# Moving two projections, their statistics and their norms by a quarter of an attention group in a four-layer kernel

## What is computed

```python
q = _split_heads(x @ Wq.T + bq)
k = _split_heads(x @ Wk.T + bk)
v = _split_heads(x @ Wv.T + bv)
scores = jnp.einsum('hbnd,hbmd->hbnm', k, q) * SCALE
attn = jax.nn.softmax(scores, axis=-1)
out = jnp.einsum('hbnm,hbmd->hbnd', attn, v)
```

## Time and profile before

| | us |
|---|---|
| median of 3 runs | 871.92 |
| lowest and highest run | 866.49, 875.07 |
| profiled execution | 876.69 |
| its span | 874.9 |

### The profile page before, as it was taken

How to read it: one execution, slowest core, us unless ns; L and a number is a source line. 1 busy time by engine, 2 the same in 40 slices (tenths; PEclk the granted TensorE clock), 3 DMA queues, 4 the chain that set the end, 5 groups by cost and what they waited for, 6 DMA issues and landing times.

```text
span 874.9 us, 13107 instructions
## 1 busy us (share of the span) xinstructions
PE 618.2 (71%) x3680; PEld 385.2 (44%) x3713; DVE 483.3 (55%) x1238; ACT 400.1 (46%) x900; POOL 365.7 (42%) x401
## 2 busy tenths in 40 slices
PE   4872109600179999930978977877978999998995
PEld 2451006300158999920968863222222233343443
DVE  4870015300036655600645677686866887867986
ACT  4420103200024666600534648555756777787651
POOL 4157750677720000075032433787477070013552
PEclk9876558855579999965879997898989999999999
DMA  8999410211102666631545645242241131000001
GB/s 270 373 247 344 169 42 1 87 54 51 48 1 72 178 172 171 180 88 42 159 119 145 166 126 150 62 138 56 52 127 54 29 104 56 1 2 0 2 12 37
DMA packets 99628, 91.52 MB, mean 105 GB/s; under 512 B 10784, under 2 KB 84608, under 8 KB 98688
## 3 DMA queue, kind: packets, MB, share of 16 engines
q1 hardware_dynamic: 90704, 75.01, 28.6%
q0 software_dynamic: 7680, 15.74, 6.2%
q10 hardware_dynamic: 1200, 0.23, 0.1%
HBM read 45.14 MB, written 45.61 MB: 104 GB/s over the span
## 4 chain that ended last, share of the span: by engine, by line
PE 46%; another core or an unknown queue 18%; DVE 14%; issue 12%; ACT 6%; DMA 2%; POOL 1%; ACTq 1%; SPq 0%; POOLq 0%; DVEq 0%
PE ps L1621 7%; PE ps L1608 6%; PE ps L1726 5%; PE ps L1736 5%; PE ps L1716 4%; DVE mx L1230 4%; PE ps L1631 3%; PE ps L1616 3%; PE ps L1530 2%; PE ps L1535 2%; ACT big L807 2%; DVE arena L1348 1%; ACT arena L773 1%; DMA dmat_s<-dmat 1%
## 5 line engine op out<-in xcount | busy, mean ns | idle before, releaser
L1230 DVE TENSOR_REDUCE mx<-ps 128x2 f32<-128x1024 f32 x128 | 151.0, 1217 | 49.5 <-PE ps L1716 37.9
L807 ACT ACTIVATE big<-ps 128x512 f32<-128x512 f32 x256 | 141.4, 598 | 67.2 <-PE ps L1726 32.7
L558 POOL DMA_INDIRECT big<-od,idx x72 | 69.0, 958 | 187.2 <-DMA od<-big 123.6
L542 POOL DMA_INDIRECT xd<-xt,idx x120 | 116.2, 968 | 69.7 <-issue 35.7
L1535 PE MATMUL ps<-arena,hmT 96*128 96x128 f32 x128 | 26.9, 343 | 125.8 <-issue 102.1
L1152 DVE TENSOR_TENSOR hm<-sg,ps 128x176 f32<-128x176 f32 x124 | 41.7, 336 | 118.1 <-ACT sg L745 74.1
L1621 PE MATMUL ps<-arena,xbT 128*128 x496 | 99.8, 325 | 4.7 <-DVE xbT L1156 2.7
L1726 PE MATMUL ps<-arena 128*128 128x512 bf16 (+1 forms) x234 | 82.6, 395 | 24.4 <-ACT big L807 11.6
L1608 PE MATMUL ps<-arena,hmT 96*128 x496 | 80.4, 286 | 26.4 <-issue 22.4
L1535 PEld LDWEIGHTS ps<-arena,hmT 96*128 96x128 f32 x128 | 21.0, 229 | 142.2 <-issue 108.0
L735 ACT ACTIVATE big<-ps 128x256 f32<-128x256 f32 x124 | 47.7, 384 | 76.2 <-PE ps L1608 47.0
(11 more groups left out here) (221 smaller groups left out, 1088.7 us busy)
## 6 DMA issues: line engine op xcount, KB each, us to landing
big<-xd SPq DMA_DIRECT2D x62, 256.0 KB
od<-big SPq DMA_DIRECT2D x62, 256.0 KB
arena<-scr SPq DMA_DIRECT2D x96, 96.0 KB
xd<-zeros SPq DMA_DIRECT2D x1, 8192.0 KB
xd<-zeros SPq DMA_DIRECT2D x1, 7680.0 KB, 30.9
arena<-w_gu SPq DMA_DIRECT2D x4, 1408.0 KB, 21.3
arena<-w_d SPq DMA_DIRECT2D x4, 768.0 KB, 17.7
scr<-places SPq DMA_DIRECT2D x8, 384.0 KB
```

Source lines behind the costliest of these rows:

```text
L542: pool.indirect_dma_start(out=xd[f], out_offset=bass.IndirectOffsetOnAxis(ap=idx[:, t, k:k + 1], axis=0), in_=xt[:, t], in_offset=None).th ...
L558: pool.indirect_dma_start(out=slot[:, k], out_offset=None, in_=od[f], in_offset=bass.IndirectOffsetOnAxis(ap=idx[:, t, k:k + 1], axis=0)). ...
L807: act.activation(ering[:, HG * (mt % 2) + h], ps[:, 4 + h % 2, :], ACT.Exp, scale=SCALE).then_inc(exp_ready, 1)
L1230: v.tensor_reduce(mx[:, k, TB * h + 2 * a:TB * h + 2 * a + 2], ps[:, 2 * a:2 * a + 2, :], AX_X, ALU.max).then_inc(s1_free, 1)
```

## The change

It moves work of sequences 2 and 3, and of those alone. Sequence 2 is projected in groups 4 and 5, sequence 3 in groups 8 and 9. "x", q, k and v each go one slot later: before (i,0) (i,1) (i,2) (i+1,0), after (i,1) (i,2) (i+1,0) (i+1,1). The statistics go from the end of the group before to behind the second row maximum of groups 4 and 8, and the norms from behind the second row maximum to behind the fifth (group 4) and the fourth (group 8). The three steps of q and of k of sequence 2 on DVE go later accordingly, and so does the DVE's copy of v. SP writes the key parts of these two sequences behind the maxima of groups 6 and 10 and no longer ahead of them. The last edit keeps PE's wait for the copied maxima in front of the first slot that is used.

```diff
--- before.py
+++ after.py
@@ -75,12 +75,15 @@
 
 
     LATER = {(0, 0): ("x", 1), (0, 1): ("q", 1), (0, 2): ("k", 1), (1, 0): ("v", 1),
-             (4, 0): ("x", 2), (4, 1): ("q", 2), (4, 2): ("k", 2), (5, 0): ("v", 2),
-             (8, 0): ("x", 3), (8, 1): ("q", 3), (8, 2): ("k", 3), (9, 0): ("v", 3)}
+             (4, 1): ("x", 2), (4, 2): ("q", 2), (5, 0): ("k", 2), (5, 1): ("v", 2),
+             (8, 1): ("x", 3), (8, 2): ("q", 3), (9, 0): ("k", 3), (9, 1): ("v", 3)}
     SLOTS = ((1, 2), (2, 2), (3, 0))
-    STATS_IN = {4: 2, 8: 3}
-    TURN_IN = {i: b for (i, _), (what, b) in LATER.items() if what == "x"}
-    PARTS_AT = ((0, 2, 1), (0, 3, 0), (0, 3, 1), (0, 3, 1), (1, 0, 0), (1, 0, 1))
+    STATS_AT = {(4, 0, 1): 2, (8, 0, 1): 3}
+    NORM_AT = {(4, 2, 0): 2, (8, 1, 1): 3}
+    V_AT = {(1, 2, 0): 1, (5, 3, 0): 2, (9, 3, 0): 3}
+    PARTS_AT = {1: ((0, 2, 1), (0, 3, 0), (0, 3, 1), (0, 3, 1), (1, 0, 0), (1, 0, 1)),
+                2: ((4, 3, 0), (4, 3, 1), (5, 0, 0), (5, 1, 1), (5, 2, 0), (5, 2, 1))}
+    WRITE_KEYS_LATER = (6, 10)
     WRITE_IN = {2: 1, 6: 2, 10: 3}
     HEAD_GROUPS = 10
     LOADS = {0: (2,), 1: (3,), 2: (4, 5), 3: (6,), 4: (7,), 6: (8, 9), 7: (10,), 8: (11,), 10: (12, 13), 11: (14,), 12: (15,)}
@@ -445,12 +448,15 @@
                 if i in WRITE_IN:
                     write_parts(sp, WRITE_IN[i], 0)
                     load_stack(sp, GB * WRITE_IN[i], 0)
-                    write_parts(sp, WRITE_IN[i], 1)
+                    if i not in WRITE_KEYS_LATER:
+                        write_parts(sp, WRITE_IN[i], 1)
                 sp.wait_ge(mT_copied, i + 1)
                 hd = HG * (i % (2 * GB))
                 if i >= 1:
                     sp.wait_ge(max_in, 16 * i)
                 sp.dma_start(kst[KM:P, hd:hd + HG, :].rearrange("p h n -> p (h n)"), mT[:, i % 2, :]).then_inc(max_in, 16)
+                if i in WRITE_KEYS_LATER:
+                    write_parts(sp, WRITE_IN[i], 1)
                 for n in LOADS.get(i, ()):
                     if n % GB:
                         load_stack(sp, n, 0)
@@ -1266,6 +1272,11 @@
                     v.wait_ge(s_r, 3 * i + 3)
                     v.tensor_tensor(mp[:, k, 2], r, mp[:, k, 1], ALU.subtract).then_inc(split_done, 1)
 
+            def late_stats(b):
+
+                v.wait_ge(summed, TB * (b + 1) - MINE - DENSE)
+                stats(tmp, B + b)
+
             def dve_group(i, k):
                 ahead = not isinstance(i, int) or i + 2 < NGR
                 after = not isinstance(i, int) or i + 1 < NGR
@@ -1276,23 +1287,24 @@
                         if after and h == 0 and a == 1:
                             copy_max(i + 1, 1 - k)
                         if isinstance(i, int):
-                            if (h, a) == (0, 1) and i in TURN_IN and i:
-                                normalise(xt, tmp, 2 * B + TURN_IN[i])
-                            if (h, a) == (2, 0) and LATER.get((i, 0), ("", 0))[0] == "v":
-                                v_in(LATER[i, 0][1], 7)
-                            for b, i0 in ((1, 0), (2, 4)):
-                                for n, place in enumerate(PARTS_AT):
-                                    if place == (i - i0, h, a):
+                            if (i, h, a) in NORM_AT:
+                                normalise(xt, tmp, 2 * B + NORM_AT[i, h, a])
+                            if (i, h, a) in V_AT:
+                                v_in(V_AT[i, h, a], 7)
+                            for b in PARTS_AT:
+                                for n, place in enumerate(PARTS_AT[b]):
+                                    if place == (i, h, a):
                                         qk_part(b, n // 3, n % 3)
+                            if (i, h, a) in STATS_AT and (h, a) != (HG - 1, 1):
+                                late_stats(STATS_AT[i, h, a])
                 out = not isinstance(i, int) or i >= 1
                 for step in range(4):
                     if ahead:
                         split_max(i + 2, k, step)
                     if out and step < 2:
                         norm_out(i - 1, 1 - k, step)
-                if isinstance(i, int) and i + 1 in STATS_IN:
-                    v.wait_ge(summed, TB * (STATS_IN[i + 1] + 1) - MINE - DENSE)
-                    stats(tmp, B + STATS_IN[i + 1])
+                if isinstance(i, int) and (i, HG - 1, 1) in STATS_AT:
+                    late_stats(STATS_AT[i, HG - 1, 1])
 
             for h in range(HG):
                 for a in range(2):
@@ -1310,7 +1322,7 @@
                         stats(tmp, B + 1)
             for step in range(4):
                 split_max(1, 1, step)
-            normalise(xt, tmp, 2 * B + TURN_IN[0])
+            normalise(xt, tmp, 2 * B + 1)
             for i in range(HEAD_GROUPS):
                 dve_group(i, i % 2)
             with v.Fori(HEAD_GROUPS // 2, NGR // 2 - 1) as j:
@@ -1835,7 +1847,7 @@
             def later_sequence(i, slot):
 
                 what, b = LATER.get((i, slot), ("", 0))
-                if what and slot == 0:
+                if what and not any((i, earlier) in LATER for earlier in range(slot)):
                     pe.wait_ge(mT_copied, i + 2)
                 if what == "x":
                     turn_in(b, ps[:, 7, :])
```

## The result

Timed beside each other, the changed kernel takes 875.15 us and the kernel before 869.62 (medians of 21 runs each): a ratio of 1.0051, 95% interval 1.0028 to 1.0073. By the ratio the change costs about half a per cent, 4.4 us, which is within 1%. The ratio is taken over undisturbed executions alone, and the two medians differ by 5.5 us. The profiled execution of the changed kernel took 877.35 us (span 875.6, mean granted clock 0.841).

A forecast was written before the change was run, and what follows sets the result against it. PE was taken to bound the kernel. Terms of +2.7 (sequence 3), +0.9 (clock), -0.4 (sequence 2) and +1.5 (clock) gave +4.7 us, moving the median from 871.9 to 876.6 us; range 865 to 885.

The forecast's parts named there:

- (A): Main case: stacks 8 and 12 land late, so PE waits ahead of groups 6 and 10; +4.7 us, chance 0.42.
- Group 8: Group 8 loses the k projection (0.9 us) and a 0.53 us row-maximum wait; waits of 0.63 and 0.55 stay.
- POOL's parts and stack 12: Group 9: parts end at 713.9, stack 12 lands 7.6 us later; PE waits 2.1 and starts group 10 2.7 late.
- Stack 8: Group 5: key parts ready after 11.5 us, stack landing at 19.5, first remote wait kept: group 6 at 658.9, -0.4 us.
- the slow subtraction: Query subtraction in group 4's last quarter, at most 2.2 us beside POOL's multiplication; move priced at zero, bounds 1.5 either way.
- Group 4 is like group 8: Group 4 was taken to shorten as group 8 does, so that group 5 begins 1.4 us earlier.
- The clock terms: Slow PE clock after idles: +0.9 us behind the wait at group 10, +1.5 behind that at group 6.
- Groups 5 and 6: Of the 7.0 us lost in group 5, the first remote wait stays and the second goes; group 6 had lost 5.0.
- Rival C: ACT's remote waits go when key writes and loads move: group 5 costs -2.4, group 6 loses 5.0; 869.6 us, chance 0.20.
- Rival B: Group 5's stalls all precede the key parts and the stack wait adds: group 6 4.6 us later; 881.6 us, chance 0.23.
- D: Stacks arrive in time, so 3.4 us of waits go as well; 868.5 us, or 861.5 without stalls; chance 0.15.
- The terms for the key parts in group 5: Fifth maximum at 8.1 us, two maxima at 1.2, rounding 0.4, last subtraction 0.7: parts ready after 11.5 us.

The follow-up runs named there:

- the kernel with both edits: Changed kernel with stacks 8 and 12 loaded with the previous sequence's keys and v copied behind the sixth row maximum; 870.58 us, 1.0022 against the kernel before.
- queries split in group 5: Changed kernel, sequence 3 in old places, group 4's norm behind fourth maximum, v's copy behind sixth, query and key steps in group 5; 871.13 us, 1.0006 to before.
- statistics alone: Kernel before with only the statistics behind the second row maximum of groups 4 and 8 and the norms behind the third; 877.62 us, 1.0102 to before.
- v copied earlier: Changed kernel with DVE's copy of v behind the sixth row maximum, not the seventh; 667.39 us, 1.0173 against the kernel before.

## Why the prediction was right, and where only its sum was

The forecast was +4.7 us; the profiles give +4.6 over the six groups, the ratio +4.4 and the medians +5.5. The mechanism of (A), two deadlines that are missed, is shown by the experiments above. The sum is closer than its terms, each of which is one trace's measure.

- **Group 8**, 15.2 us forecast: 15.09. The 0.53 for the row maximum went; the wait for x (0.51) and for ACT ahead of the turned outputs (0.55) stayed, as said.
- **POOL's parts and stack 12.** POOL began 6.8 us after group 9's start (702.40 to 709.20); the forecast came out at 6.9. From write to landing it was 7.0 and not 7.6, and the hold was 0.64 and not 2.1, half because of that and half because PE came later to it: v's copy cost 1.47 in place of 1.1, and 0.42 stood ahead of a score matmul, with ACT's exponentials late behind its copies of k, which I had not counted. Groups 8 and 9 together cost 1.87 us, 2.7 forecast. In a series of waits their sum is set by the last one; the size of the first only moves the share.
- **Stack 8.** The group was forecast at 21.5 us (to 658.9) and took 21.34, by another way. ACT's remote wait, 4.0 us before, was absent; in its place the write left 14.9 us into the group and not 11.5. The fifth row maximum began 9.9 us into the group where I had put 8.1, and DVE's last step took 2.35 us where I had put 0.7. The late maximum alone is enough for the missed deadline: in the changed kernel of the 656 us series the step takes 0.68 us, but the fifth maximum begins 10.7 us into the group, the write leaves at 14.1, and the hold is 2.96 us. I had seen the slow subtraction and priced its move at zero: this term was mis-sized too. The Trainium skill (SBUF — State Buffer, Who interferes with whom) has a VectorE instruction with two SBUF inputs contend with a GpSimd instruction that reads SBUF, where the order of issue decides which one blocks. The 2.35 us step, which began 0.10 us behind POOL's multiplication, agrees with that. The 3.05 us step does not: by its row it began 0.58 us ahead of POOL's and still ended behind it, and the measurement decides. I had applied the rule only to the end of group 9.
- **Group 4**, 15.2 us forecast by "Group 4 is like group 8": 17.96. This step failed. The norm stands behind the fifth maximum here and behind the fourth in group 8, so PE waits 1.79 us for x and not 0.6, which is 1.2 of the 2.8 us. The other 1.6 is the clock: the kernel with both edits, with the same wait and a clock of 1.00, takes 16.38 us. With the norm behind the fourth maximum the same group takes 15.1 us (queries split in group 5), as forecast.
- **The clock terms**, +0.9 and +1.5, did not come where they were put: behind the holds of 0.64 and 1.98 us the clock stayed at full speed. It fell in group 4 instead, where no term stood. The size was partly misread as well: the pair of scores of 0.88 us ran at a granted clock of 1.00 (before, 648.5 to 649.5), and a like pair stands at full clock in group 9 (709.66 above); a slow pair takes 1.03 to 1.09 us.
- **Groups 5 and 6.** I kept the first remote wait of group 5, dropped the second, and left the loss of group 6 as it was. In group 5 both are absent; group 6 takes 17.85 us for 17.14, 5.7 over group 7, with this one in it, and behind it a slow stretch (from ACT's timeline):

```profile
667.87 2.32 ACT L813 ACTIVATE big<-ps 128x512 f32<-128x512 f32 x4 [3.78 <-remote]
```

- **Rival C** says that ACT's remote waits go with the move. The one of group 5 did, but the kernel with both edits, whose key write also stands behind the maxima of group 6, has one of 3.90 us there, which ends 2.2 us ahead of that write (649.0 and 651.3), the one with the queries spread has none, and all kernels of the 871 us series have one in group 6. In the kernel before of the 656 us series the key write (at 440.51) and its loads run among gathers in group 5 with no such wait, so they alone do not make it. What does is not settled. **Rival B**'s added stall did not occur, and **D** fell with the waits on the stacks.

The terms for the key parts in group 5 add to 11.6 and not 11.5, which changes nothing. That the sum came out is thus partly luck: groups 4 to 6 cost 2.85 us where 1.1 was forecast, groups 8 and 9 cost 1.87 where 3.6 was, clock terms included.

## What to carry to other kernels

Work that runs ahead of its use has a deadline; before it is moved later, count the whole chain to that deadline (split, write, DRAM, load: 6.4 to 7.3 us for the DMAs alone in the changed kernel), and not the engine that does it. Two waits in a row on the engine that bounds the kernel must be removed together, since one alone gives back little or nothing. A short VectorE step on such a chain should not stand where GpSimd's long elementwise instruction falls, which cost it 1.7 to 2.4 us here. Doing the three steps in a row as soon as the keys were there brought the write 3.1 us forward.

## What the runs showed that was not expected

**200 us ahead of the attention.** The same kernel takes 656 us in one series and 871 in the other, and both were seen on one chip. The loss stands between 90 and 240 us of the span. One window of each, before in the 871 us series and then in the 656 us one (there, PE works on in the same stretch):

```profile
90.00:240.00 150.00, 43.63 (x212) 30.38 (x214) 24.03 (x128) 20.41 (x53) 90.90 (x95) 0.60 0.17 59
```

```profile
90.00:240.00 150.00, 147.20 (x1081) 131.57 (x1082) 87.94 (x280) 85.12 (x262) 107.43 (x105) 1.00 0.62 183
```

In the slower one engines stand for some 16 us at a time:

```profile
106.66 0.38 ACT L709 ACTIVATE hmT<-ps 96x256 f32<-96x256 f32 x1 [16.48 <-remote]
```

What releases them is not in the trace, and its cause is open. It is why comparisons were made within a series only.

**The clock after an idle.** It fell behind waits of 1.79 us (changed, group 4), 2.37 (queries split, group 6), 2.94 (statistics alone) and 7.00 (v copied earlier). It did not fall behind waits of 1.98 (changed, group 6) and 2.96 us (changed, 656 us series), nor behind the same wait of 1.79 us in the same place in the kernel with both edits. The length of the one wait before it does not tell whether the clock falls.

**DVE beside POOL.** The step of 0.68 us took 2.35 and 3.05 us beside POOL's multiplication of 1.9 us. In the second case DVE began 0.58 us ahead of POOL (443.19 against 443.77) and still ended 0.56 behind it (446.24 against 445.68). All twelve slow subtractions of groups 4 and 5 beside this multiplication, in ten traces, end 0.55 or 0.56 us after it, whichever of the two began first.
